# Two slot tables of a windowed local attention: value projections, and the norm of the fourth key tile, at other slots

## The reference, cut to what matters

```python
h = shift_token(x)
q, k, v = split(h @ wqkv)                 # 128 -> 3 * 512, 8 heads of 64
q = l2norm(q) * qs;  k = l2norm(k) * ksc
q, k = rotary_xpos(q, k)                  # q*cos*scale + rotate_half(q)*sin*scale
o = local_attention(q, k, v)              # window of 64, and the 64 keys before it
x = x + o @ wo
h = (layernorm(shift_token(x)) * lg + lb) @ w1 + b1
a, g = split(h)
x = x + (a * gelu(g)) @ w2 + b2
```

## Time and profile before

| | |
|---|---|
| median of 3 runs | 4819.50 us (4791.46 to 4824.86) |
| profiled execution | 4808.8 us, span 4807.0 us |
| TensorE matmul busy | 4240.2 us, 88% of the span |
| VectorE busy | 2952.2 us, 61% |
| ScalarE busy | 2457.1 us, 51% |
| GpSimd busy | 1127.4 us, 23% |
| granted clock of TensorE, mean | 0.894 of full speed |
| local attention, first time (first score to last) | 526.6 us |
| local attention, second time | 513.2 us |

### The profile page before, as it was taken

One profiled execution on the slowest core, in us unless ns is written; L12 is line 12 of the kernel. 1 busy time (PEld: TensorE's weight loads), 2 busy tenths in 40 slices (PEclk: granted clock), 3 DMA queues, 4 the chain that ended last, 5 costly groups with the idle time before them and its releaser, 6 DMA issues.

```text
span 4807.0 us, 64297 instructions
## 1 busy us (share of the span) xinstructions
PE 4240.2 (88%) x24136; PEld 2036.5 (42%) x24136; DVE 2952.2 (61%) x6570; ACT 2457.1 (51%) x4189; POOL 1127.4 (23%) x1587
## 2 busy tenths in 40 slices
PE   7888879999898889999886778899888999889999
PEld 4222345665531236555553224555553334333343
DVE  5888465656478866666345994666666653466632
ACT  3577634454348774554345553454444663236642
POOL 1000123333210013333112662111122003420034
PEclk9799987788879997988888998999997999969999
DMA  1100102111010011111000000000001000000000
GB/s 50 27 17 12 45 24 53 27 34 36 6 53 21 15 44 37 36 32 30 5 7 5 0 0 16 8 16 8 16 29 30 21 8 0 29 22 21 15 1 9
DMA packets 48023, 104.18 MB, mean 22 GB/s; under 512 B 15064, under 2 KB 15064, under 8 KB 46432
## 3 DMA queue, kind: packets, MB, share of 16 engines
q1 hardware_dynamic: 46560, 98.49, 7.5%
q10 hardware_dynamic: 1152, 1.57, 0.1%
HBM read 40.24 MB, written 1.05 MB: 9 GB/s over the span
## 4 chain that ended last, share of the span: by engine, by line
PE 66%; DVE 20%; ACT 7%; POOL 3%; issue 2%; ACTq 1%; DMA 0%; SPq 0%; POOLq 0%; DVEq 0%
PE PS L446 31%; PE PS L1122 8%; PE PS L1070 7%; DVE SM L1196 6%; PE PS L1102 3%; PE PS L2629 2%; DVE AR L2433 2%; ACT AR L453 2%; DVE AR L450 2%; PE PS L1753 1%; PE PS L1798 1%; PE PS L1743 1%; PE PS L473 1%; PE PS L1075 1%; ACT AR L1170 1%
## 5 line engine op out<-in xcount | busy, mean ns | idle before, releaser
L1196 DVE TENSOR_REDUCE SM<-PS 128x1 f32<-128x512 f32 (+3 forms) x1792 | 1028.7, 626 | 239.0 <-PE PS L1070 158.9
L446 PE MATMUL PS<-AR,WS 128*128 128x512 f32 (+1 forms) x2112 | 1063.2, 643 | 70.3 <-DVE AR L450 26.3
L1170 ACT ACTIVATE AR<-PS 128x1024 f32<-128x1024 f32 (+3 forms) x896 | 825.4, 933 | 338.5 <-PE PS L1105 169.2
L453 ACT ACTIVATE AR<-PS 128x512 f32<-128x512 f32 (+4 forms) x728 | 442.6, 615 | 537.1 <-PE PS L446 404.0
L1070 PE MATMUL PS<-AR 51*128 51x512 bf16 (+3 forms) x1792 | 526.9, 390 | 143.5 <-DVE SM L1196 98.8
L446 PEld LDWEIGHTS PS<-AR,WS 128*128 128x128 f32 (+1 forms) x2112 | 403.5, 202 | 526.4 <-issue 408.4
L1821 ACT ACTIVATE AR<-PS,SM 128x128 f32<-128x128 f32 x512 | 229.6, 452 | 471.5 <-DVE SM L1884 469.2
L1122 PE MATMUL PS<-AR 128*32 128x512 f32 (+3 forms) x3584 | 447.6, 572 | 1.3 <-ACT AR L1170 0.9
L1070 PEld LDWEIGHTS PS<-AR 51*128 51x128 bf16 x1792 | 129.9, 94 | 660.3 <-DVE SM L1196 476.6
L1102 PE MATMUL PS<-AR 51*128 51x512 bf16 (+3 forms) x1792 | 386.9, 367 | 11.8 <-ACT AR L1170 11.0
L1229 POOL CAST MBT<-SM 128x8 bf16<-128x8 f32 x128 | 28.0, 219 | 1256.6 <-DVE SM L1200 1051.6
(11 more groups left out here) (322 smaller groups left out, 7241.2 us busy)
## 6 DMA issues: line engine op xcount, KB each, us to landing
TP<-RAW SPq DMA_DIRECT2D x512, 64.0 KB, 2.0
AR<-AR SPq DMA_DIRECT2D x720, 32.0 KB
WS<-wall SPq DMA_DIRECT2D x4, 3654.5 KB, 11.2
WS<-wall SPq DMA_DIRECT2D x8, 902.5 KB, 4.5
WS<-wall SPq DMA_DIRECT2D x2, 3334.5 KB, 10.5
WS<-wall SPq DMA_DIRECT2D x1, 2384.0 KB, 9.5
WS<-wall SPq DMA_DIRECT2D x1, 1543.5 KB, 6.2
AR<-AR ACTq DMA_DIRECT2D x48, 32.0 KB
```

The costliest lines, as they stand in the source:

```text
L446: t = e.matmul(o, l, r, start=(n == 0), stop=(n == len(pairs) - 1))
L453: return e.activation(o, i, ACT.Copy, scale=1.0)
L1170: e.activation(pv[:, :, off:512], sv[:, :, off:512], ACT.Exp, scale=scale).then_inc(*F.at_exp.up((s, u, p2)))
L1196: e.tensor_reduce(mh[:, at, k0 // 512:k0 // 512 + 1], bank(ring(n + g), m), AX.X, ALU.max, negate=True).then_inc(*F.at_max.up((s, k, i, rr ...
```

## The change

Two entries of the tables move in every group, and with the first of them the three slots in which the key root takes its steps. In group 0's own slots the value table stays as it was. Gate, up and down stay where they were.

```diff
-                second = [("norm", g, j) for j, at in enumerate((2, 3, 4, 4, 6, 7, 10, 11)) if n == at] + second
+                second = [("norm", g, j) for j, at in enumerate((2, 3, 4, 5, 6, 7, 10, 11)) if n == at] + second
...
-                second += [("v", g, j) for j, at in enumerate((8, 11, 14, 15) if g else (8, 11, 12, 12)) if n == at]
+                second += [("v", g, j) for j, at in enumerate((11, 12, 13, 15) if g else (8, 11, 12, 12)) if n == at]
...
-                if g < 8 and n in (5, 6, 7):
+                if g < 8 and n in (6, 7, 8):
                     next(roots[g, 1], None)
```

## The result

The changed kernel took 4853.55 us (median of 6 runs, 4846.93 to 4871.50), against 4820.27 us of the kernel before in its 6 runs: a ratio of 1.0083, with a 95% interval of 1.0061 to 1.0104. It is slower by 0.8%. Forecast were 4812 us and no change. The profiled execution took 4851.46 us, 42.7 us more than that of the kernel before, to which the forecast had added 4.

What follows compares the result with a forecast made beforehand. TensorE was taken to bound the two local attention stages, with gains only in its clock and few waits. The terms, -24 - 7 + 3 + 8 + 24 = +4 us on the profiled 4808.8, gave 4812 us, range 4768 to 4856.

Steps and rivals of the forecast that it cites:

- Term 1: Slots 5 and 6: with the norm moved, a group's first drop to half clock is gone; 24 us less.
- term 3: Slot 6: the norm at its end newly waits for VectorE's key-norm maximum; 0.2 us a group, 3 us more.
- the second fall: The later of two drops to 1.2 GHz in a group, in slot 13; 54 us in all before the change.
- Term 2: Slots 12 and 13: moved value projections partly fill TensorE's wait for VectorE; 0.5 us a group, 7 us less.
- Term 4: Slot 8 of groups 0 and 1, left without dense items: longer half clock, 2 us a group, 8 us more.
- Term 5: Slots 13 to 15, into 0 and 1: the half clock stays and lasts longer, 1.7 us a group, 24 us more.
- The slower rival: Half clock lasts into slots with norms, some 10 us lost a group instead of 4.2; 4865 us, chance 0.14.
- a sign of a wrong prediction: Slots 11 to 13 already at half clock, or slots 14 and 15 at 1.00, would show the forecast wrong.

Runs made afterwards that it cites:

- Norm and root alone: Kernel before with only the norm of the fourth key tile and the key root moved, value projections left in place: 4781.11 us, ratio 0.993.
- Either half alone: Two kernels, each the kernel before with one part moved: norm and key root, 4781.11 us; value projections, 4852.73 us.
- the kernel with the doubled projection: Whole change, but the third value projection computed in slot 13 and once more in slot 14: 4867.63 us, ratio 1.0095.
- (8, 11, 13, 15): Kernel before with norm and key root moved, and of the value projections only the third, from slot 14 to 13: 4837.41 us, ratio 1.0041.
- (11, 12, 14, 15): Kernel before with norm and key root moved, the value projection of slot 8 gone from there, that of slot 14 kept: 4838.81 us, ratio 1.005.

## Why the prediction was wrong

**Term 1, right.** With the norm's move slots 5 and 6 keep full clock in all groups 1 to 6: they take 3.49 and 3.82 us, forecast were 3.5 each. In three of the ten groups 2 to 6 a fall comes two slots later, in slot 7, which takes 9.56 instead of 8.21. Over slots 4 to 9 of these ten groups the time at half clock went from 47.8 to 10.2 us, a gain of some 19 us. Norm and root alone gave 31 us, not 24 less the 3 of term 3: the second fall became shorter too, without being touched.

**Term 2, right in its course, of no weight.** The step that VectorE sets was read rightly, the wait of the third spreading came, at 1.49 us (1.8 forecast), and slots 12 and 13 at full clock took 3.47 and 5.02 in group 5, together 8.5 (8.2 forecast). The second gap was not there; the term had the fourth spreading wait once more behind the transposes.

**Term 3, right.** Slot 6 takes 3.82 instead of 3.50, 0.3 a group against 0.2. The wait shows as the norm's later start.

**Term 4, the first wrong size.** It priced the empty slot 8 of groups 0 and 1 at 8 us; they took 23.5 more. It looked at group 1 for the loss, but group 0 had it, 79.01 us twice. Either half alone gave 66.8 to 71.1 us. That the two act together is not shown: the kernel with the doubled projection has the same work there up to slot 13, and group 0 took 78.9 us in its first stage and 70.8 in its second.

**Term 5, the step that failed.** "So I take the fall as staying, 2 to 3 us later": in group 4 it came in slot 11 instead of slot 13, and so in six of the ten groups 2 to 6. In slots 10 to 15 and 0 to 3 of groups 2 to 6 the time at half clock went from 125.1 to 191.2 us. Half of the 66 us is what it costs: 33 us in ten groups, against the 1.7 a group, 17, that the term allowed. What it had right is the part on slot 14: without its projection the clock comes back later, which the run with (8, 11, 13, 15) shows by itself. What it left out is the other end of the same move. It looked only at the stretch between the projections of slots 12 and 13, and at slot 14. That slot 8 lost its projection had a price in groups 0 and 1 alone (term 4), and none in groups 2 to 6. There slot 11, whose own items were not touched, lost the clock in six or seven groups of ten in every kernel without that projection.

The slower rival had this ("If the clock is lost in slot 11"), at 0.14. Its 4865 us lie nearer to the 4853.55 measured than the forecast does, but by another sum: it had 5.8 us more a group, and the fourteen groups lost 2.7 each in the mean. In part the forecast was also low by its base. It started from the profiled 4808.8 us, 11 below the median, and 4.6 of the 42.6 us between the spans came outside the fourteen groups. What was named as a sign of a wrong prediction, half clock in slots 11 to 13, is there.

The prediction drew on the Trainium skill, TensorE: Matmul & The Clock Gate, section "Why this matters for your kernels", for its advice against idle gaps of TensorE. That advice is for longer gaps than the 2.00 us of slot 13, so it does not say what this gap costs. Here filling the gap with two products kept the clock in six of ten groups. The advice was no guide for slots 5 and 11, which fell with TensorE busy all the time (3.94 of 3.94 us, and 4.70 of 4.70 above).

**What stays open.** Why slot 11 falls when slot 8 has lost its projection, with slots 9 and 10 between them at full clock, is not shown. Nor is it the whole cause. Slots 10 and 11 hold the same items in all these kernels. The clock fell in slot 11 in no group before, in one of the ten groups 2 to 6 with norm and root alone, in three with (8, 11, 13, 15), in six with the change and in six with (11, 12, 14, 15). In the changed kernel group 4 fell and group 5 did not. It may also hang on when a group reaches the slot, which moves with every fall and return before it. No run here fixed that moment, so what a given table does in a given group was not predictable from these runs.

## What to carry to other kernels

Where TensorE bounds a stage and its granted clock changes within it, a move of full-size products is to be judged from both ends: what it fills, and what it empties. A projection that is put behind a wait is not in the wait; it must be issued ahead of the waiting instruction, and without making another instruction wait for its bank. Try each part of a change alone: here one half was worth 0.7% and the other cost more than that.

## What was not expected of the hardware

- Useless work made the kernel faster: 28 products of 0.86 us, in all 24 us at full clock, took the kernel before from 4815 to 4774 us (ratio 0.9915, 0.9885 to 0.9945).
- The half clock can last long with TensorE at work: group 0 at 0.50 for 79.01 us, TensorE busy for 77.70 of them; in another kernel 48 us in group 1.
- A slot whose instructions and order are untouched takes 2.64 or 4.54 us (slot 15), by what the slots ahead of it did to the clock.
